# Turning gathered token rows with a transposing DMA instead of TensorE and VectorE, in a two-layer mixture-of-experts kernel on one core

## What is computed

```python
w, sel = jax.lax.top_k(probs, K)            # K = 2 of 8 experts
Wte = Wte.at[jnp.arange(T)[:, None], sel].add(w)
for i in range(sh_gate.shape[0]):           # 2 shared experts, all tokens
    shared = shared + _swiglu(x, sh_gate[i], sh_up[i], sh_down[i])
for e in range(exp_gate.shape[0]):          # 8 routed experts
    routed = routed + Wte[:, e:e + 1] * _swiglu(x, exp_gate[e], exp_up[e], exp_down[e])
out = shared + SCALE * routed               # _swiglu: silu(x @ wg) * (x @ wu) @ wd, F = 352
```

## Time and profile before

| | us |
|---|---|
| median of three runs | 402.48 |
| the three runs | 402.94, 396.69, 402.48 |
| profiled execution, its own time | 396.08 |
| its span on the core | 394.3 |
| PE busy | 366.0 (93%) |
| DVE busy | 252.2 (64%) |
| ACT busy | 166.6 (42%) |
| POOL busy | 138.3 (35%) |

### The profile page before, as it was taken

The page is one execution under the profiler, slowest core; times in us unless marked ns, Lnnn a source line. Parts: engine busy times, 40 slices in busy tenths (PEclk is TensorE's granted clock), DMA queues, the critical chain, the costliest instruction groups (busy, mean ns, idle before and its releaser), DMA issues.

```text
span 394.3 us, 7801 instructions
## 1 busy us (share of the span) xinstructions
PE 366.0 (93%) x2671; PEld 223.2 (57%) x2672; DVE 252.2 (64%) x619; ACT 166.6 (42%) x287; POOL 138.3 (35%) x129
## 2 busy tenths in 40 slices
PE   7998996998999999966999899999999999999992
PEld 2344443453455454522655577777777777776561
DVE  1368999998755655788735365555555555546574
ACT  1145254647567557525324033333333333333460
POOL 3000252521535322000100145555555555521643
PEclk9999999899999999998999999999999999999997
DMA  7965231323433510000000022222222222213922
GB/s 236 390 256 197 71 93 59 132 72 125 141 107 121 155 59 23 25 30 0 2 27 1 15 64 78 77 77 80 80 80 80 80 80 80 80 41 97 352 112 107
DMA packets 18037, 39.24 MB, mean 100 GB/s; under 512 B 2976, under 2 KB 9376, under 8 KB 17888
## 3 DMA queue, kind: packets, MB, share of 16 engines
q1 hardware_dynamic: 13552, 28.71, 21.7%
q0 software_dynamic: 3744, 10.23, 8.4%
q10 hardware_dynamic: 720, 0.02, 0.1%
HBM read 29.65 MB, written 9.31 MB: 99 GB/s over the span
## 4 chain that ended last, share of the span: by engine, by line
PE 71%; DVE 19%; ACT 3%; issue 3%; DMA 2%; POOL 1%; POOLq 0%; ACTq 0%; SPq 0%; DVEq 0%
PE bank L993 56%; PE bank L1140 7%; PE bank L1237 3%; DVE x L772 3%; PE bank L1221 2%; PE bank L1009 2%; DVE prod L898 2%; DMA x<-wc 2%; DVE x L886 1%; DVE w0s L642 1%; ACT acts L577 1%; DVE oh L682 1%; DVE hs L630 1%; DVE acts L903 1%; ACT sil L567 1%
## 5 line engine op out<-in xcount | busy, mean ns | idle before, releaser
L993 PE MATMUL bank<-w0s,hs 128*128 128x512 f16 x384 | 87.6, 383 | 5.5 <-DVE x L772 4.6
L437 POOL TENSOR_TENSOR w1s<-piece,w1s 128x1360 f16<-128x1360 f32 x16 | 44.3, 2779 | 102.8 <-ACT piece L526 102.8
L993 PE MATMUL bank<-w1s,rT 128*128 x468 | 76.2, 313 | 1.5 <-DVE rT L957 1.5
L446 POOL DMA_INDIRECT rows<-token_store,row_in x39 | 37.9, 971 | 94.8 <-PE bank L1221 49.9
L993 PE MATMUL bank<-hs,w1s 128*128 128x512 f16 x264 | 61.0, 386 | 6.3 <-DVE prod L898 6.3
L993 PEld LDWEIGHTS bank<-w0s,hs 128*128 128x128 f16 x384 | 37.1, 99 | 49.5 <-DVE x L772 6.2
L772 DVE SCALAR_TENSOR_TENSOR x<-bank,coef,x 128x256 f32<-128x256 f32 x128 | 54.4, 477 | 15.8 <-PE bank L993 15.4
L993 PEld LDWEIGHTS bank<-w1s,rT 128*128 128x128 f16 x468 | 44.0, 98 | 22.0 <-issue 2.0
L451 POOL DMA_INDIRECT results<-yb,row_out x39 | 38.5, 987 | 37.0 <-ACT yb L601 37.0
L993 PEld LDWEIGHTS bank<-hs,w1s 128*128 128x128 f16 x264 | 25.2, 99 | 37.5 <-DVE prod L898 8.6
L993 PE MATMUL bank<-w1s,aT 128*128 (+1 forms) x351 | 44.8, 272 | 0.8 <-DVE aT L950 0.8
(11 more groups left out here) (149 smaller groups left out, 423.6 us busy)
## 6 DMA issues: line engine op xcount, KB each, us to landing
piece<-w SPq DMA_DIRECT2D x16, 680.0 KB, 3.9
w1s<-results SPq DMA_DIRECT2D x6, 512.0 KB, 9.2
x<-wc SPq DMA_DIRECT2D x4, 512.0 KB, 6.7
w1s<-xT SPq DMA_DIRECT2D x4, 512.0 KB, 10.3
w1s<-w SPq DMA_DIRECT2D x4, 512.0 KB, 8.9
token_store<-xrow SPq DMA_DIRECT2D x4, 512.0 KB, 2.9
out<-x SPq DMA_DIRECT2D x8, 256.0 KB, 2.3
x<-x SPq DMA_DIRECT2D x1, 1536.0 KB, 10.6
```

Of the source, the lines that this page charges most:

```text
L437: nc.gpsimd.tensor_tensor(w1s[:, LO, i * PIECE:(i + 1) * PIECE], piece[:, i % 2], w1s[:, HI, i * PIECE:(i + 1) * PIECE], ALU.subtract).the ...
L446: pool.indirect_dma_start(rows[:, i % 2], None, token_store, bass.IndirectOffsetOnAxis(row_in[:, i:i + 1], 0)).then_inc(s_row[i % 2], 16)
L993: mm = nc.tensor.matmul(out_ap, l, r, start=(i == 0), stop=(i == len(terms) - 1))
```

## The change

The four transposes and the copy to `rT` are dropped, with the semaphores `s_ra` and `s_rx`. In their place SyncE issues, for each of the 39 tiles, one transposing DMA of `rows[:, i % 2]` (128 partitions x 512 fp16, 128 KB) into `rT[:, i % 2]`, signalled on `s_turn`. It waits for the gather of tile i (`s_row`) and, from the third tile on, for the up product of tile i-2 (`s_ru`). The gather of tile i now waits for the landing of the transposing DMA of tile i-2. Gate and up wait for `s_turn`, and for the product of tile i-2 (`s_rprod`), which has read the banks that they write. The wait ahead of the loop is for the shared products (`s_prod`) instead of `s_acc`.

```diff
@@ sync
             keep(2)
             keep(3)
 
+            for i in range(TILES):
+                sp.wait_ge(s_row[i % 2], landed(i, i % 2))
+                if i >= 2:
+                    sp.wait_ge(sm["s_ru"], i - 1)
+                sp.dma_start_transpose(rT[:, i % 2].rearrange("p a k n -> p (a k) n"), rows[:, i % 2]
+                                       ).then_inc(s_turn[i % 2], 16)
 
             sp.wait_ge(s_put[0], 16 * ((TILES + 1) // 2))
@@ gpsimd
             def fetch(i):
                 if i >= 2:
-                    pool.wait_ge(sm["s_ra"], i - 1)
+                    pool.wait_ge(s_turn[i % 2], landed(i - 2, i % 2))
@@ vector, step
-                i = s + 2
-                if known(i):
-                    dve.wait_ge(sm["s_ra"], i + 1)
-                    if again(i):
-                        dve.wait_ge(sm["s_ru"], i - 1)
-                    nc.vector.tensor_copy(rT[:, par].rearrange("p a k n -> p (a k n)").bitcast(F32),
-                                          bank[4][:, 0:D]).then_inc(sm["s_rx"], 1)
@@ tensor, step
-                i = s + 2
-                if known(i):
-                    pe.wait_ge(s_row[par], landed(i, par))
-                    if isinstance(i, int) and i == 1:
-                        pe.wait_ge(sm["s_rx"], i)
-                    for a in range(2):
-                        for k in range(KT):
-                            o = (a * KT + k) * P
-                            mm = nc.tensor.transpose(bank16[4][:, o:o + P], rows[:, par, o:o + P], ident16[:])
-                    mm.then_inc(sm["s_ra"], 1)
...
-                    pe.wait_ge(sm["s_rx"], i + 1)
+                    pe.wait_ge(s_turn[par], landed(i, par))
+                    if again(i):
+                        pe.wait_ge(sm["s_rprod"], i - 1)
                     for g, done in enumerate(("s_rg", "s_ru")):
@@ tensor, ahead of the loop
-            pe.wait_ge(sm["s_acc"], TPB + 1)
+            pe.wait_ge(sm["s_prod"], EARLY)
```

More of the change, by code:

```diff
@@ L253, in build_program @@
             "s_acc",
-            "s_ra",
-            "s_rx",
             "s_rg",
@@ L281, in build_program @@
         s_row = [sem(f"s_row{c}") for c in range(2)]
+        s_turn = [sem(f"s_turn{c}") for c in range(2)]
         s_put = [sem(f"s_put{c}") for c in range(2)]
```

## The result

The changed kernel takes 415.08 us (median of 4 runs, 413.44 to 420.44) against 400.41 for the kernel before in the same comparison: ratio 1.0385, 95% interval 1.0254 to 1.0515. The forecast was 393.0; the time lies in the range (386.5 to 428), but the kernel became slower where it was forecast to become faster. An execution of one and the same kernel sometimes falls into a slower state, as the one at 420.44 did; medians here hold all runs, ratios and intervals only those in the faster state.

What follows compares the result with a forecast made beforehand. TensorE was taken to bound the routed loop. An earlier tile 2 (227.1) plus 36 periods of 3.116 us ends at 339.3 against 348.79: -9.5 us, so 402.48 - 9.5 = 393.0 us, range 386.5 to 428.

Steps and rivals of the forecast that it cites:

- TensorE sets the pace, and 0.22 us a tile is the price of the transposes: Routed loop: dropping row transposes cuts TensorE's period from 3.336 to 3.116 us, 7.9 us less over 36 periods.
- Head of the loop: Loop start: gate and up of tile 0 start at 222.05 instead of 223.12, tile 1 at 223.84, tile 2 at 227.1.
- The copy on DVE is worth nothing; SyncE has room: Loop: DVE's dropped 424 ns copy saves no time; SyncE's 39 issues, 0.33 to 1.02 us each, fit into a period.
- L, the transposing DMA: Latency of the DMA into rT, from its waits being met to its landing: taken as 3.0 to 3.3 us.
- may cost it some tenths more: Gather and scatter bursts of 0.4 to 0.8 us on the DMA engines could lengthen the transposing DMA by tenths.
- so G = 2.3 us: Gather's time, from POOL's instruction start at 271.20 to its data's end at 273.5.
- the formula: Period P of the loop through two rows buffers: 2P >= L + 2.8, so beyond the limit P = (L + 2.8) / 2.
- The form of the loop: Through two rows buffers, a gather waits for tile i's transposing DMA, whose successor waits for that gather.
- its warning sign: POOL's gathers released by the transposing DMA, starting about 2.8 us before the next one of the same buffer is issued.
- the threshold: Largest transposing-DMA latency L at which TensorE's period of 3.116 us still holds: 3.4 us.
- slower: Rival, 0.36: L exceeds 4.3 us, gate and up wait for s_turn; +11 us at L = 4.5, +100 at 9.2.
- inside the loop TensorE alone sets the pace: Steady routed loop, 235 to 340 us: TensorE busy throughout, so removing its instructions shortens the loop unless something else becomes later.

Runs made afterwards that it cites:

- e5: Changed kernel with four row buffers instead of two and without the scatters of tiles 0 to 36: 388.54 us, ratio 0.9751 to the kernel before.
- e7: Changed kernel with gathers for the first two tiles only, later transposing DMAs reading a token tile of xrow, scatters kept: 388.21 us, ratio 0.972.
- e3: Changed kernel without the scatters of tiles 0 to 36, loads behind the loop reading input instead: 394.01 us, ratio 0.9893 to the kernel before.
- e1: Changed kernel with four buffers for the gathered rows instead of two, nothing else: 416.11 us, ratio 1.0448 to the kernel before.
- e2: Changed kernel with an ordinary copy of the same 128 KB in place of the transposing DMA: 412.49 us, ratio 1.0416 to the kernel before.
- e4: Kernel before with 39 transposing DMAs of the same size added on SyncE, into a spare tile nobody reads: 405.97 us, ratio 1.0184.
- e11: Kernel before with scatter and gather swapped in POOL's list, each gather directly behind a scatter, no transposing DMA: 413.79 us, ratio 1.0374.
- e13: Kernel before with scatter and gather swapped in POOL's list, plus a 256-column POOL memset ahead of each: 414.0 us, ratio 1.0374.
- e10: Changed kernel with four row buffers, each gather from the fifth on held back until DVE's product of tile i-3: 410.18 us, ratio 1.0246.
- e9: Changed kernel with four row buffers, each gather from the fifth on held back until the up product of tile i-3: 400.01 us, ratio 1.0029.
- e12: e9 plus a 128-column POOL memset ahead of every gather and scatter: 404.52 us, ratio 1.0139 to the kernel before.
- e15: e1 plus a 256-column POOL memset ahead of each gather and scatter: 399.89 us, ratio 1.001 to the kernel before.

## Why the prediction was wrong

*TensorE sets the pace, and 0.22 us a tile is the price of the transposes*: right. `e5` and `e7` run at 3.117 and 3.115 against the forecast 3.116, their 388.5 and 388.2 us are ratios of 0.975 and 0.972, and -9.5 us on 402.48 is 0.976.

*Head of the loop*: right. Gate and up of tile 0 follow the last shared down product, and tile 2 comes 4.66 us later; the forecast had 5.05.

*The copy on DVE is worth nothing; SyncE has room*: right. An issue took 1.19 us, above both my prices of 0.33 and 1.02, and still fitted into a period.

*L, the transposing DMA*: 2.48 us undisturbed, below my 3.0 to 3.3, and 3.43 in the loop, just over 3.4. I had written that bursts "may cost it some tenths more"; they cost 0.9, and `e3` has it back at 2.44 by taking the scatters away. The page "Advanced Engine Details and Errata" of the Trainium skill, section "X-Bar Transpose (TRN2)", has such DMAs as fast as plain ones; for one transfer of 128 KB the trace does not agree, with 0.78 us of data against 0.51, 1.19 us of issuing against 0.465 and a landing of 2.43 us (`e1`) against 1.88 (`e2`). The Trainium skill's 1309 ns a block, from "VectorE: DVE Perf Modes", section "The three transpose paths", is not a rate here: four blocks landed in 2.48 us.

*"so G = 2.3 us"*: this is the step that failed. I took the gather from POOL's start to the last byte in the GB/s row of the kernel before, and used that in a loop with other traffic. G measured 3.84 in the changed kernel's chain, 1.5 more. With G = 2.3 the formula at L = 3.43 gives (3.43 + 2.3 + 0.47) / 2 = 3.10 and TensorE stays in charge; with the measured 3.84 and handoffs of 0.28 it gives 3.78.

The 1.5 us have two parts. A landing ends with its completion, which has no bytes to see. In the kernel before, the gather of 271.20 has its last completion packet at 273.60 and the last recorded update of its semaphore at 273.73, 2.53 us after its start; the median of 30 is 2.52. That part is 0.2 us, and with G = 2.52 the formula still gives 3.12. The rest came with the change. The loop starts each gather together with a transposing DMA, and the scatter follows 1.28 us later. A gather started at 292.31 there had its last completion packet at 295.33 (3.02 us later), and SyncE was released at 295.85, 0.5 us after that; the median of the recorded landings is 3.56. I had allowed L some tenths for such traffic, and G nothing. That it is the traffic, and not the gather, `e3` (2.75), `e1` (2.74) and `e4` (3.20) show.

The form of the loop was right, and so was its warning sign, gathers released by the DMA. With the measured G the threshold was not L = 3.4 but L = 6.23 - 3.84 - 0.28 = 2.1, below even the undisturbed landing. The rival that was called *slower* has the result, but its condition, L above 4.3, was not met: in the chain L stays between 3.29 and 3.60. That the time fell into the stated range is owed to the wide upper end, not to the sum.

*"inside the loop TensorE alone sets the pace"*: incomplete. It holds for the kernel before, and `e11` shows that it needs POOL's order there. In the kernel before, the gather's wait for `s_ra`, four transposes at the start of a step, put it 1.55 us or more from either scatter. I had priced the transposes as work and never as what paced POOL's queue. Replacing that wait by one on `s_turn` put 30 pairs under 1.4 us. This second limit is hidden behind the first in the changed kernel (10 signals are late there, eight of them by 0.5 us or less, and one `sil`), and it is why four buffers alone, which my formula would have called the cure, gained nothing.

What stays open: how POOL's indirect DMAs hold up TensorE's signals. That close pairs bring late signals is shown by `e11` against `e13` and by `e10` against `e9`. That distance is not all of it is shown by `e12` and `e15`, which have late signals with no pair under 1.45 and 1.58 us and the transposing DMA beside them, by `e4`, and by the close pairs that did no harm. Whether the signals are late themselves or wait in a common path was not tried.

## What to carry to other kernels

When a wait on compute becomes a wait on a DMA, write down every loop of landings through the buffers, and price each landing from issue to the start of its waiter, never from the bytes. Price it in the traffic of the new loop: a loop that starts two transfers together makes both longer. An instruction that is removed may also have been what spaced another queue: look at who waited for it and where that one starts now. And when one of two limits is taken away without effect, take both limits away together before giving up the theory.

## What the runs showed of the hardware

The signal of TensorE's up product came 3.6 to 3.7 us after the group's start instead of 1.97, at full granted clock and with the group's matmuls recorded as long as ever (1.95 us), in 13 of 36 tiles when a gather started on POOL 1.3 us behind a scatter (`e11`); at 1.6 us apart, in the same order, none was late (`e13`). Both kernels take 3.7% longer than the kernel before, so the late signals alone do not account for it.

Beside another transfer's packets the completions took longer than the data. The transposing DMA issued at 292.35 had moved its 512 packets of 256 bytes between 293.52 and 294.36; its completion packets are recorded from 294.70 to 295.34, between those of a gather, and POOL was released at 295.98. Undisturbed, data and completions together took from 229.11 to 230.03. For so small a transfer the data is a small part of L: 0.84 us of the 3.63 from issue to release.
